# Expert tiles of the first eight batches start while the last batches are still routed

## The reference, cut to what matters

```
x = x + xattn(layernorm(x), ctx, ctx)      # 8 heads of 32, decayed scores in the mLSTM form, a norm per head
xn = layernorm(x)
s  = xn @ gate_w.T                         # 8 experts
top2 of s, softmax over the two            # per token: two experts, two probabilities
x  = x + sum_k p_k * ( silu(xn@w1[e]) * (xn@w2[e]) ) @ w3[e]    # hidden 512
```

## Time and profile before

| | us |
|---|---|
| median of three runs | 658.14 |
| the profiled execution | 654.9 |
| its span | 653.1 |
| last value matmul of mixing starts | 226.44 |
| first product of the first expert tile starts | 290.22 |
| TensorE busy, share of the span | 86% |
| VectorE, ScalarE, GpSimd busy | 69%, 53%, 45% |

### The profile page before, as it was taken

The page is one execution under the profiler, slowest core; times in us unless marked ns, Lnnn a source line. Parts: engine busy times, 40 slices in busy tenths (PEclk is TensorE's granted clock), DMA queues, the critical chain, the costliest instruction groups (busy, mean ns, idle before and its releaser), DMA issues.

```text
span 653.1 us, 14222 instructions
## 1 busy us (share of the span) xinstructions
PE 564.8 (86%) x3612; PEld 466.0 (71%) x3613; DVE 451.9 (69%) x987; ACT 348.5 (53%) x769; POOL 296.5 (45%) x312
## 2 busy tenths in 40 slices
PE   3779879999989951239999999999999999999993
PEld 1334668888878840127888888888888888888882
DVE  4664586787777778946667677667767767767762
ACT  2456556777777755014555555555555555555551
POOL 5423136365455534032555555555555555555532
PEclk9899998999999955559999999999999999999998
DMA  7875336787776668921433333333333333433322
GB/s 231 252 225 162 91 93 185 200 212 197 210 219 172 193 161 244 279 50 17 66 50 50 62 51 50 62 52 50 62 52 50 59 54 49 59 55 49 59 40 24
DMA packets 66018, 73.44 MB, mean 112 GB/s; under 512 B 12762, under 2 KB 55776, under 8 KB 65984
## 3 DMA queue, kind: packets, MB, share of 16 engines
q0 software_dynamic: 18240, 28.17, 25.1%
q1 hardware_dynamic: 38528, 36.21, 19.1%
q10 hardware_dynamic: 9216, 8.65, 3.9%
HBM read 43.51 MB, written 19.01 MB: 96 GB/s over the span
## 4 chain that ended last, share of the span: by engine, by line
issue 40%; POOL 15%; PE 14%; DVE 14%; DMA 10%; ACT 4%; SPq 1%; ACTq 0%; DVEq 0%; POOLq 0%
POOL xg L1168 9%; DMA out_rows<-ys,index 6%; PE bank L1287 5%; POOL out_rows L1177 4%; PE dots L1269 3%; DVE ohn L996 2%; DMA w12h<-in_x 2%; DVE ohp L995 2%; DVE c L846 1%; DVE st L727 1%; PE dots L1222 1%; ACT x2n L636 1%; PE bank L1336 1%; PE dots L1220 1%; DVE tot L887 1%
## 5 line engine op out<-in xcount | busy, mean ns | idle before, releaser
L1177 POOL DMA_INDIRECT out_rows<-ys,index x71 | 112.5, 1585 | 156.1 <-DVE ys L1048 145.1
L1054 DVE TENSOR_TENSOR w3l<-w,w3h 128x1024 fp32r<-128x1024 f32 x71 | 87.2, 1229 | 30.9 <-issue 29.7
L1168 POOL DMA_INDIRECT xg<-token_table,index x71 | 70.4, 992 | 46.1 <-DVE index L1013 24.4
L693 ACT CAST w3h<-w 128x1024 fp32r x71 | 74.4, 1048 | 20.4 <-issue 20.4
L1409 PE MATMUL bank<-w3l,hth 128*128 128x256 f32 x284 | 76.5, 302 | 1.8 <-DVE w3l L1054 1.8
L1410 PE MATMUL bank<-w3h,hth 128*128 128x256 f32 x284 | 70.8, 282 | 0.0
L1287 PE MATMUL bank<-aug,c 128*128 128x99 f32 (+2 forms) x512 | 63.9, 279 | 6.0 <-DVE c L846 5.9
L1287 PEld LDWEIGHTS bank<-aug,c 128*128 128x128 f32 x512 | 60.8, 195 | 11.0 <-DVE c L846 10.3
L1048 DVE TENSOR_SCALAR ys<-bank,pc 128x256 f32<-128x256 f32 x71 | 34.4, 484 | 46.6 <-PE bank L1413 46.6
L1031 DVE TENSOR_TENSOR htl<-bank,hth 128x512 fp32r<-128x512 f32 x71 | 49.1, 692 | 25.2 <-ACT hth L683 25.2
L1381 PE MATMUL weighs<-w12l,xh 128*128 x144 | 62.3, 432 | 1.1 <-DVE xl L1020 1.1
(11 more groups left out here) (172 smaller groups left out, 1235.1 us busy)
## 6 DMA issues: line engine op xcount, KB each, us to landing
w12l<-in_w12T SPq DMA_DIRECT2D x24, 256.0 KB, 3.5
aug<-in_ctxv SPq DMA_DIRECT2D x16, 264.0 KB, 3.5
w12h<-in_x SPq DMA_DIRECT2D x16, 256.0 KB, 3.6
w12l<-in_ctxT SPq DMA_DIRECT2D x16, 256.0 KB, 3.6
qbd<-w12h SPq DMA_DIRECT2D x64, 64.0 KB
x<-in_x SPq DMA_DIRECT2D x16, 256.0 KB, 3.3
out_rows<-x ACTq DMA_DIRECT2D x16, 256.0 KB, 2.5
token_table<-x2n ACTq DMA_DIRECT2D x16, 256.0 KB, 3.5
```

Source lines behind the costliest of these rows:

```text
L693: nc.scalar.copy(W3H[i][:], w3[:, bass.ds(e, 1)].rearrange("p a k d -> p (a k d)")).then_inc(w3h_ready, 1)
L1054: v.tensor_tensor(W3L[i][:], w3[:, bass.ds(e, 1)].rearrange("p a k d -> p (a k d)"), W3H[i][:].bitcast(F32), ALU.subtract).then_inc(w3l_re ...
L1168: q.indirect_dma_start(out=XG[x][:], out_offset=None, in_=table, in_offset=bass.IndirectOffsetOnAxis(ap=index[:, j:j + 1], axis=0)).then_i ...
L1177: q.indirect_dma_start(out=out, out_offset=bass.IndirectOffsetOnAxis(ap=index[:, j:j + 1], axis=0), in_=YS[o][:], in_offset=None, compute_ ...
```

## The change

The routing table is made in parts, and its first part early.

- **Groups.** The 16 batches form five groups: 0-2, 3-5, 6-7, 8-11, 12-15. Each group's choice, ranks and slots are computed on their own. `seen` carries the counts of the groups before. A slot is the expert's number times 4096 plus the rank, in a DRAM table `places` of pairs (token, probability).
- **Placement.** For each 128 pairs GpSimd issues an indirect transfer of 8 bytes per row into `places` (`place`). 32 of them are issued in batches 8 to 14, 4 in tiles 1 and 2, 12 in tiles 4 to 9, 16 in tiles 11 to 18.
- **Lists.** After the eighth batch the number of full tiles of each expert is known; at least 25 are full. `fetch_list` gathers the rows of `places` that make the first 25 tiles, TensorE turns them, VectorE takes `index`, `prob` and `etab`. The other 46 tiles get a second list in tiles 19 to 21.
- **Remains.** What mixing had left after batch 15 (the rows, gate scores and the choice of batches 12 to 15) is done by functions `remains(j)` inside the expert tiles 0 to 21, on TensorE, ScalarE and VectorE. ScalarE changes its function table for it at tiles 2, 5 and 9, and back.
- **Weights.** The last 8 pieces of w12 are loaded and split in batches 4 to 7; three pieces (batches 13 to 15) are subtracted by VectorE. w3 isn't kept: SyncE loads the 512 KB of a tile's expert for each tile, two tiles ahead, and no probability is stored in `token_table`.
- **SyncE** issues the values and kn ahead of the x rows.
- **Loops.** Mixing and the first 28 tiles are written out, all tiles on VectorE.

The core of the diff:

```diff
+CUT = B // 2
+FIRST = (CUT * S * TOPK - NE * (P - 1) + P - 1) // P
+GROUPS = ((0, 3), (3, 6), (6, CUT), (CUT, 12), (12, B))
-ROW = E + NE
+ROW = E
...
+            def load_w3(j, i):
+
+                wait(sp, w3l_ready, j - 1)
+                e = sp.value_load(etab[0:1, bass.ds(j, 1)], min_val=0, max_val=NE - 1)
+                sp.dma_start(W3[i][:], w3T[:, bass.ds(e * (KH * E), KH * E)]).then_inc(w3_in[i], 16)
...
+            def place(g, lo, hi):
+
+                k0 = group(g)[2]
+                pool.wait_ge(slots_ready, g + 1)
+                pool.wait_ge(pairs_ready, g + 1)
+                for k in range(k0 + lo, k0 + hi):
+                    q.indirect_dma_start(out=places, out_offset=bass.IndirectOffsetOnAxis(ap=slot[:, k:k + 1], axis=0),
+                                         in_=pairs[:, k, :], in_offset=None).then_inc(placed, 16)
+
+            def fetch_list(ph):
+
+                w = LISTS[ph][2]
+                pool.wait_ge(row_ready, 2 * ph + 2)
+                pool.wait_ge(placed, 16 * TOPK * NT // 2 * (ph + 1))
+                q.indirect_dma_start(out=listed[0:w].rearrange("p s c -> p (s c)"), out_offset=None, in_=place_rows,
+                                     in_offset=bass.IndirectOffsetOnAxis(ap=rowid[0:w, ph:ph + 1], axis=0)
+                                     ).then_inc(list_in, 16)
...
+                if b in (8, 9, 10):
+                    place(0, 4 * (b - 8), 4 * (b - 7))
+                if b in (11, 12):
+                    place(1, 6 * (b - 11), 6 * (b - 10))
...
+                if j in (2, 5, 9):
+                    nc.scalar.preload_act_table_set("natural_log_exp_and_others")
+                if j == 2:
+                    row_scales(B - 2)
+                    head_scales(B - 1)
...
+                if j in (1, 2):
+                    place(3, 2 * (j - 1), 2 * j)
+                if 4 <= j < 10:
+                    place(3, 2 * (j - 2), 2 * (j - 1))
+                if 11 <= j < 19:
+                    place(4, 2 * (j - 11), 2 * (j - 10))
+                if j == 19:
+                    fetch_list(1)
...
+            def ranks(g, to):
+
+                _, nt, _ = group(g)
+                W = nt * NE
+                pe.wait_ge(r_ones, g + 1)
+                mm(to[:, 0:W], tri[:, 0, :], abf[:, 0:W], start=True, stop=False)
...
+                for gr, (lo, hi) in enumerate(GROUPS[:3]):
+                    if b == hi + 4:
+                        pe.wait_ge(kvb_ready, HG * (b + 1))
+                        ranks(gr, bank[6][:, 384:512])
```

More of the change, by code:

```diff
@@ L229, in build @@
-        YS = [sb(f"ys{i}", [P, E], on=f) for i in range(2)]
-        PC = [sb(f"pc{i}", [P, 1], on=f) for i in range(NX)]
         f.close()
@@ new lines, in near, with state @@
+            def near(b):
+                act.wait_ge(pv_group, NC * b + 1)
+                wait(act, x2_ready, b - 1)
+                nc.scalar.copy(TOT[b % 2][:, 0:NH, :].rearrange("p h d -> p (h d)"),
+                               bank[4][:, 0:NH * DV]).then_inc(o0_taken, 1)
+            def state(b, i):
+                act.wait_ge(kv_psum, b + 1)
+                wait(act, inter_ready, b - 1)
+                for j in range(HG):
+                    lo, hi = j * DH, (j + 1) * DH
+                    kv = bank[6][lo:hi, 0:NG * HG * DV].rearrange("p (n j d) -> p n j d", n=NG, j=HG)
+                    nc.scalar.mul(KVB[i][lo:hi, :, j, :], kv[:, :, j, :], KS).then_inc(kvb_ready, 1)
@@ new lines, in odds @@
+            def odds(g):
+                nt = group(g)[1]
+                act.wait_ge(r_diff, g + 1)
+                nc.scalar.activation(ex[:, 0:nt], diff[:, 0:nt], ACT.Exp).then_inc(r_exp, 1)
+            weights(0, 0)
+            for b in range(B):
+                i = b % 2
+                if has(b, 1):
+                    near(b - 1)
+                state(b, i)
+                if has(b, 3):
+                    turned(b - 3)
+                weights(b, 1)
+                if b == 0:
@@ L1012, in _ @@
-            st.then(v.scalar_tensor_tensor(count[:], token, -1.0, wrap[:], ALU.add, ALU.add))
-            v.tensor_tensor(index[:], count[:], fil[:], ALU.add).then_inc(tables, 1)
+                if has(b, 1):
+                    variances(b - 1, X2N[1 - i][:].rearrange("p c (h d) -> p (c h) d", h=NH))
+                if has(b, 2):
+                    row_means(b - 2)
+                if b == 1:
+                    three_parts(dve, v, negM, REST, m_parts, 2 * PARTS - 1, 0, PARTS)
+                if has(b, 3) and b < B - 1:
+                    take_scores(b - 3, SCORES)
@@ L1056, in _ @@
+            last_low(B - 3)
+            last_low(B - 2)
+            take_scores(B - 4, SCORES)
+            last_low(B - 1)
+            far(B - 1)
             low(0, 0)
-            dve.wait_ge(w3_in, 16 * NE)
-            dve.wait_ge(tables, 1)
-            expert_tiles(dve, expert)
+            for j in range(TILES + 1):
+                expert(j, j % 2)
         @block.gpsimd
@@ L1166, in gather @@
                 wait(pool, xt_psum, j - NX + 1)
[L1167 to L1168 removed]
+                q.indirect_dma_start(out=XG[x][:], out_offset=None,
+                                     in_=table[0:CUT * S, :] if j < FIRST else table,
                                      in_offset=bass.IndirectOffsetOnAxis(ap=index[:, j:j + 1], axis=0)
```

1102 lines of the change are left out of this document (627 added, 475 removed).

## The result

The changed kernel took 678.93 us (median of 4 runs, 674.18 to 684.44), the kernel before 657.69 beside it: ratio 1.030, 95% interval 1.022 to 1.039. Some runs fall in a slower state of the chip; they are in the medians but not in the ratios, so a ratio here can differ from the quotient of two medians, by up to 0.011. The forecast was 638, with a range to 661. The profiled execution has a span of 674.6 us (653.1 before).

A forecast was written before the change was run, and what follows sets the result against it. TensorE and VectorE were taken as nearly full in mixing, VectorE's routing chain as the gap's bound, TensorE as the expert stage's. 654.9 - 52 + 16 + 17 = 636, set at 638 toward the runs' median; range 616 to 661.

The forecast's parts named there:

- The gap (-52): Between mixing and the first expert product: the early list lets that product follow a short chain, 52 us sooner.
- GpSimd in a batch: Mixing: GpSimd's busy sums with placements exceed VectorE's longer batches only in batches 11 to 13, +2.5 us.
- VectorE's steps (+15.5): Mixing: 66 small steps between VectorE's two halves of the scores, at 0.235 us each, add 15.5 us.
- ranks (+3): Mixing: TensorE's ranks wait for ScalarE's copy of the state, about 1 us three times, +3 us.
- pieces (+1): Batches 4 to 7: the late w12 pieces' extra transfers bring the DMA share to about 1, +1 us.
- SyncE's order (-6): Mixing: kn arrives earlier, so batches 4 to 15 come 6 us sooner.
- GpSimd has 2.1 us idle per tile: Expert stage: two placements put GpSimd 0.5 us behind per tile in 16 tiles, mostly within a 5 us allowance, +1.
- The rest of this stage (+16): Expert stage without GpSimd's part: TensorE's added work +6.5, ScalarE's table loads and waits +9.3, VectorE +1.5, written-out loops -1.
- Placements cost as much as scatter-adds: Rival, 10%: at 1.9 us a placement, GpSimd slows batches 8 to 14 and tiles 1 to 18; 666 us.
- All hidden: Rival, 15%: VectorE's and ScalarE's additions fall into idle time in mixing and the expert stage; 616 us.
- The hand-over is late: Rival, 14%: waits in program order pile up in batch 15, or batches 4 to 7 lose time, another 15 us; 653.
- w3 comes too late: Rival, 7%: in the expert tiles each w3 load takes over 7 us to land; 675 us.

The follow-up runs named there:

- the quiet kernel: The kernel before with SyncE's order alone changed, values and kn loaded ahead of the rows of x: 652.60 us, ratio 0.994.
- the reordered kernel: The change with VectorE's steps and TensorE's ranks later, placements ahead of the weighing, squares in their own buffer, ScalarE's piece work earlier: 670.72 us, ratio 1.016.

## Why the prediction was wrong, step by step

- **The gap (-52): right in size, in part by luck.** -50.4. The chain has the forecast members in the forecast order, and the price of a placement was right: 1.04 us and 0.30 of issue, forecast 1.0 and 0.3. But counted as in the forecast, from the end of the weighing for batch 15 (251.3) to the first product, it took 24.0 us, not 18.9: the list's gather went out 5.3 us after the last placement's issue, not 2.8, and from first gather to first product it was 6.9, not 4.8. It doesn't show in the gap, since the values of batch 15 came 6.2 us behind the weighing, not 3.0. Three edges of the chain (weighing, list, first gather), then the prices:

```profile
250.70 0.62 POOL L1283 TENSOR_TENSOR vw<-aug,cols 128x264 f32<-128x264 f32 x1 [1.10 <-DMA kn<-in_ctx]
...
259.42 0.89 POOL L1321 DMA_INDIRECT listed<-slot_table,rowid  x1 [4.37 <-DMA slot_table<-pairs,slot]
...
268.39 1.04 POOL L1363 DMA_INDIRECT xg<-token_table,index  x1 [2.92 <-DVE clear L1007]
```

```profile
L1373 POOL DMA_INDIRECT out_rows<-ys,index x71 | 143.1, 2016 | 107.2 <-DVE ys L1175 60.7
...
L1313 POOL DMA_INDIRECT slot_table<-pairs,slot x64 | 66.4, 1038 | 18.5 <-issue 17.7
```

- **The step that failed in mixing** is "GpSimd in a batch: ... together 5.2; with 4, 6, 5 placements 10.4, 13.0, 11.7 ... so only batches 11 to 13 stand out: +2.5". The busy times were right; what failed is taking the longer of two busy sums for the length of a batch. By the traces the early placements cost 16.1 us (143.5 against 127.4), by the ratios some 19; taking for each of batches 8 to 14 the longer of GpSimd's sum and its length without placements would have given some 5 (an estimate). One thing left out is that GpSimd's idle time has a fixed place, in front of the weighing (48.7 us of waiting for kn in 11 batches, called "mostly unseen by TensorE" in the same term). In order, batch 11 is 4.4 of wait plus 13, not 13. In the quiet kernel work behind the weighing cost 14.2 us where the same work ahead of it cost 8.0. The other is the waiting and the lower clock that even well-placed work brings in a loop that isn't quiet: ahead of the weighing the placements still cost 8.6 us of batches 8 to 15 (88.0 against 79.4, 6.0 of it TensorE's busy time, at a clock of 0.86), and 10.1 of mixing in the reordered kernel. So roughly half is the place. How the cost divides in the change itself rests on single traces.
- **VectorE's steps (+15.5), ranks (+3) and pieces (+1), 19.5 in all: too small, 24.5.** That is what mixing without early placements (127.4) has over the quiet kernel (102.9). Two sizes were off. In the quiet kernel a step that makes TensorE wait cost 0.39 us, not 0.235, since the lower clock came behind the wait; this I hadn't in the sum at all, though the earlier trace rows show the clock at 0.52 in the idle gap. How much of the 24.5 it makes wasn't measured in the change. And of the late pieces I priced the transfers (1 us), not ScalarE's two roundings and negation, which stand in front of the copy that TensorE's values wait for: 10.9 us instead of 9.35 in batches 4 and 5, light loads or not, and 9.4 in batch 4 with that work moved in ScalarE's order or to GpSimd. The waits of TensorE's ranks for ScalarE's copy were three of 2.7 us on average (8.2 in all), not of 1.
- **SyncE's order (-6): right**, -5.9 alone. In the change it can't be seen, since GpSimd is late by itself.
- **The step that failed in the expert stage** is "GpSimd has 2.1 us idle per tile, two placements cost 2.6: it falls behind 0.5 a tile in 16 tiles ...: +1". It costs 16.1. The 2.07 of the earlier trace rows hold 0.30 of issue that isn't free, so the lag is 0.9 a tile; the 5 us of allowance are used up after six tiles; and waits for SyncE's permission (up to 3.2 us) come in between, in which nothing queued behind can run. The lag then falls on TensorE and at the end on the second list. In the reordered kernel the same placements made 22.2 us.
- **The rest of this stage (+16): nearly right**, 20.3 without late placements. Tiles 3, 6 and 10, forecast at 8 us, took 8.6, 9.0 and 8.0. ScalarE in the first of them, from the cast of w3 to Silu:

```profile
292.93 1.05 ACT L775 CAST w3h<-w3raw 128x1024 fp32r<-128x1024 f32 x1
294.00 1.28 ACT L785 ACT_TABLE_LOAD   x1
295.29 0.29 ACT L534 ACTIVATE lnv<-mv,eps 128x2 f32<-128x2 f32 x1
...
297.10 1.28 ACT L760 ACT_TABLE_LOAD   x1
298.39 0.60 ACT L760 ACTIVATE sg<-dots 128x512 f32<-128x512 f32 x1
```

The two table loads took 1.28 us, as in the earlier trace rows, and stand within 0.03 us of the operations on both sides. The drain of about 1380 ns that the Trainium skill (ScalarE: Activation LUTs, What ACT_TABLE_LOAD costs) has beside the load isn't seen; here the measurement decides. By the Trainium skill's sum, an estimate, the six switches would have made these tiles some 8 us longer.
- **Rivals.** "Placements cost as much as scatter-adds" had the right places, and at 666 it was nearer than the forecast, for a wrong reason: a placement cost 1.04 us, not 1.58, and its share came from the order and the loop around it. "All hidden" is out: even without early placements mixing took 127.4 us. "The hand-over is late" is out where it named batch 15 (17.8 us to the first product, 16 forecast); batches 4 to 7, its other place, were 9.3 us longer than before, but with ScalarE's work and not the transfers as a cause where it was tried. "w3 comes too late" is out: loads landed after 3.8 us, tiles 23 and later take 4.96.
- **What stays open.** Why single traces of the same mixing differ by 10 us; the clock's dips make small delays large, but what starts them in one run and not in another wasn't tried. Nor was why late placements cost more in the other traces (up to 407.1 us of expert stage) than in the change's own. And of the reordered kernel's 122.5 us of mixing, 20 over the quiet kernel, I haven't told VectorE's part from ScalarE's by an experiment in it.

Reordered and without placements, a kernel that leaves out part of the work, the change reached 636.8 us. That this is near the forecast of 638 doesn't make the forecast right. The idea is sound here as far as TensorE, VectorE and ScalarE go; what sinks it is 64 placements of 1.3 us on GpSimd: by the quiet kernel and one trace of the change, about half of their cost in mixing comes from standing behind a wait that they could fill, the rest from their time alone. Putting them ahead of it didn't shorten the run.

## What to carry to other kernels

For an engine that gets more work, don't compare busy sums with the period: write its period in program order, with its waits at their places, and ask of each wait whether the new work stands on the side that can fill it. Price a new long stall of TensorE above its own length: here one of 4.6 us cost 7.9, while stalls of 1.2 us, one a batch, left the clock at 1.00. When a bundle of edits includes one that is cheap to try alone, as SyncE's order was, try it alone: it was the part that won.

## What the runs showed of the hardware

- After TensorE had waited 4.6 us its clock stood at 0.50 (1.2 GHz) for some 7 us (an estimate from four rows of 2 us: 0.59, 0.50, 0.50, 0.71), with TensorE busy throughout, and returned to 1.00. In the kernels with GpSimd's added work it fell after waits of 2.72 and 1.75 us and not after seven waits of 0.5 to 1.2 us.
- Placements (128 rows of 8 bytes each) leave GpSimd after 1.04 us, but stores of rows beside them land after 8.2 us instead of 4.8 and kn after 7.6 instead of 4.1.
- Scatter-adds took 2.02 us on average instead of 1.58, and 2.07 in the kernel without any placement; which of the changes (the w3 loads among them) does it wasn't tried.
